# Splitting the second mixture's second-layer weights in two halves: four chunks beside the last attention batch, four in its tail

## The reference, cut to what matters

```python
x = x + L1_xattn(layernorm(x), ctx, ctx)     # 16 heads of 16: scores, softmax, values, output projection
x = x + L1_ffn(layernorm(x))                 # mixture of 8 experts, one expert per token
# inside L1_ffn, for the expert idx of each token:
h = gelu(x @ W1[idx] + b1[idx])              # W1: 8 x 256 x 512
o = (h @ W2[idx] + b2[idx]) * score          # W2: 8 x 512 x 256
```

## Time and profile before

| | |
|---|---|
| three timed runs | 1160.39, 1146.82, 1158.53 us (median 1158.53) |
| profiled execution, its own time | 1146.98 us |
| its span in the trace | 1145.2 us |
| PE, DVE, ACT, POOL busy | 85%, 65%, 42%, 25% of the span |
| chain that ended last | PE 49%, DVE 27%, DMA 10%, ACT 6% |
| mean granted TensorE clock | 0.919 of full |
| last attention batch and its tail, gate and routing | about 914 to 1040 us of the span |

### The profile page before, as it was taken

How to read it: one execution, slowest core, us unless ns; L and a number is a source line. 1 busy time by engine, 2 the same in 40 slices (tenths; PEclk the granted TensorE clock), 3 DMA queues, 4 the chain that set the end, 5 groups by cost and what they waited for, 6 DMA issues and landing times.

```text
span 1145.2 us, 20649 instructions
## 1 busy us (share of the span) xinstructions
PE 975.3 (85%) x6905; PEld 588.1 (51%) x6905; DVE 742.6 (65%) x1952; ACT 478.4 (42%) x1055; POOL 283.5 (25%) x248
## 2 busy tenths in 40 slices
PE   6878789878898799999998876888989897877993
PEld 3555455646465388878885432333333332335662
DVE  3474677684978766666663467687677856446665
ACT  3443725442343334433442310446665666532331
POOL 0334434523320233444321111100010011112551
PEclk8999989997998899999999997779998998887997
DMA  9442020003435311111114486323073014061225
GB/s 290 148 129 95 16 72 4 19 1 92 130 110 166 128 65 51 48 53 49 52 40 147 122 148 122 74 39 75 2 120 65 3 57 128 20 201 34 79 76 175
DMA packets 69506, 98.64 MB, mean 86 GB/s; under 512 B 6528, under 2 KB 56960, under 8 KB 66976
## 3 DMA queue, kind: packets, MB, share of 16 engines
q1 hardware_dynamic: 59808, 62.18, 19.0%
q0 software_dynamic: 9600, 35.14, 12.0%
HBM read 70.10 MB, written 27.13 MB: 85 GB/s over the span
## 4 chain that ended last, share of the span: by engine, by line
PE 49%; DVE 27%; DMA 10%; ACT 6%; issue 4%; POOL 2%; SPq 1%; DVEq 0%; POOLq 0%; ACTq 0%
PE pb L993 11%; PE pb L1010 7%; DVE MX L1932 5%; PE pb L1098 4%; PE pb L1011 3%; DMA QS<-qd 3%; PE pb L1122 3%; PE pb L758 2%; PE pb L1076 2%; PE pb L827 2%; PE pb L781 2%; PE pb L837 2%; DMA xr<-rows,gi 2%; DVE TQ L1541 1%; PE pb L1153 1%
## 5 line engine op out<-in xcount | busy, mean ns | idle before, releaser
L1355 ACT ACTIVATE m<-pb,b1m 128x128 f32<-128x128 f32 x404 | 115.1, 368 | 172.2 <-PE pb L993 172.1
L1932 DVE TENSOR_REDUCE MX<-pb 128x1 f32<-128x512 f32 x256 | 158.6, 684 | 43.7 <-PE pb L1076 43.3
L1412 ACT ACTIVATE EX<-pb 128x512 f32<-128x512 f32 x256 | 136.9, 598 | 115.4 <-PE pb L1122 114.5
L993 PE MATMUL pb<-xt,w1h 128*128 128x128 f16 x1616 | 157.6, 221 | 3.9 <-issue 2.7
L1010 PE MATMUL pb<-w,mh 128*128 x404 | 149.5, 380 | 5.4 <-DVE ml L1843 4.9
L752 PE MATMUL pb<-identh 128*128 128x512 f16 x558 | 136.6, 401 | 15.5 <-DVE UZ L1577 8.8
L993 PEld LDWEIGHTS pb<-xt,w1h 128*128 x1616 | 120.3, 98 | 42.5 <-issue 6.1
L993 PE MATMUL pb<-xt,w1l 128*128 128x128 f16 x808 | 112.8, 221 | 0.0
L1011 PE MATMUL pb<-w,ml 128*128 x404 | 110.2, 273 | 0.0
L2144 POOL DMA_INDIRECT outs<-ob,di x62 | 61.4, 990 | 174.3 <-DVE ob L1858 174.3
L752 PEld LDWEIGHTS pb<-identh 128*128 128x128 f16 x558 | 55.4, 102 | 87.4 <-issue 18.9
(11 more groups left out here) (319 smaller groups left out, 1598.0 us busy)
## 6 DMA issues: line engine op xcount, KB each, us to landing
SR<-in_w1m SPq DMA_DIRECT2D x20, 512.0 KB, 4.3
SR<-in_w2m SPq DMA_DIRECT2D x14, 512.0 KB, 4.8
GB<-outs SPq DMA_DIRECT2D x12, 512.0 KB, 6.9
KS<-kd SPq DMA_DIRECT2D x48, 128.0 KB, 5.6
QS<-qd POOLq DMA_DIRECT2D x24, 256.0 KB, 10.1
SRW<-in_w2m SPq DMA_DIRECT2D x10, 512.0 KB, 5.3
kd<-KHL POOLq DMA_DIRECT2D x8, 512.0 KB, 6.6
vd<-VAB POOLq DMA_DIRECT2D x4, 1024.0 KB, 4.4
```

The lines of the kernel that those rows point to most:

```text
L993: ins = pe.matmul(k.ap[:, h4 * TOK:(h4 + 1) * TOK], wt[:, bass.ds(regs[j], 128)], M.xt[j % 2][:, xc, :], start=i == 0, stop=i == 5)
L1355: ins = act.activation(M.m32[x % 2][:, h4, :], k.ap[:, h4 * TOK:(h4 + 1) * TOK], M.func, bias=M.b1[:, bass.ds(reg + 4 * g + h4, 1)], scale ...
L1412: act.activation(EX[m % len(EX)][:, i, :], k.ap, ACT.Exp, scale=0.25).then_inc(k.out, 1)
L1932: v.tensor_reduce(mx[:, t, 2 * s + j:2 * s + j + 1], k.ap, AX.X, ALU.max).then_inc(k.out, 1)
```

## The change

The chunks of `o` are taken in another order: those of w_1_2 and w_1_3 first, then those of w_1_0 and w_1_1. The first four use only the two staging buffers of the even batches, and go beside the last attention batch, behind the split `n` (nine steps: one to start and two for each chunk). SP waits for the last attention output only ahead of the fifth chunk. The other four begin after eight steps of the tail of batch 3, where the whole split began after two before.

```diff
--- before.py
+++ after.py
@@ -390,13 +390,16 @@
         def shaped(buf, like):
             return buf if len(like.shape) == 2 else buf.rearrange("p (e n) -> p e n", e=like.shape[1])
 
+        def back_first(xs):
+            return xs[len(xs) // 2:] + xs[:len(xs) // 2]
+
         def turn(n, k):
             return [i % k for i in range(n)]
 
         splits = dict(a=(cut(*W1x, a["W1T"].rearrange("p c n -> p (c n)")) + cut(*W2x, a["W2T"].rearrange("p c n -> p (c n)")), SR0, turn(4, 3)),
                       m=(blocks(E0.w1h, E0.w1l, a["w1m0"]), SR + SRS, turn(8, 3) + [3, 4, 5, 0, 1, 2, 5, 0]),
                       p=(blocks(E0.w2h, E0.w2l, a["w2m0"]), SRW + SR, [4, 5, 3, 0, 1, 2, 4, 5, 3, 0, 1, 2, 0, 1, 2, 0]),
-                      n=(blocks(E1.w1h, E1.w1l, a["w1m1"]), SR1, turn(8, 2)), o=(blocks(E1.w2h, E1.w2l, a["w2m1"]), SR2, turn(8, 4)))
+                      n=(blocks(E1.w1h, E1.w1l, a["w1m1"]), SR1, turn(8, 2)), o=(back_first(blocks(E1.w2h, E1.w2l, a["w2m1"])), SR2, [0, 1, 0, 1, 2, 3, 0, 1]))
 
         chunk_dma, chunk_at, slot_of, loaded_chunks, split_chunks = {}, {}, {}, {}, 0
         for tag in "ampno":
@@ -494,7 +497,7 @@
                 for b in bs:
                     yield from p["gate"](b)
 
-            tails = {}
+            tails, down = {}, p["split"]("o")
             for b in range(NB):
                 if 1 <= b < NB - 1:
                     p["load_half"](b + 1, 1)
@@ -504,14 +507,11 @@
                 beside(p["attend"](b, tails),
                        (chain(tails[b - 1] if b else nothing(), p["load_v"](b + 1) if 1 <= b < NB - 1 else nothing(),
                               p["qprep"](b + 2) if b + 2 < NB else nothing(),
-                              p["split"]("n") if last else nothing()), 1.0 if b else 1.3),
+                              chain(p["split"]("n"), islice(down, 9)) if last else nothing()), 1.0 if b else 1.3),
                        (gates(range(NB - 1)) if last else chain(nothing() if b else m0, p["maxima"](b + 1, b + 2 if b + 2 < NB else None)),
                         1.1 if b else 1.6))
             p["attend_done"]()
-            down = p["split"]("o")
-            for _ in range(2):
-                next(tails[NB - 1])
-            next(down)
+            weave(islice(tails[NB - 1], 8))
             beside(chain(tails[NB - 1], gates([NB - 1])), (down, 0.3), drain=False)
             p["route"](R1)
             ex = p["experts"](E1)
@@ -584,19 +584,21 @@
                         w.wait_ge(*lo_token("m", (12, 13, 15)[i]))
                     if tag == "p" and i == 3:
                         w.wait_ge(sem("x1"), NB)
+                    if tag == "o" and i == 4:
+                        w.wait_ge(bO.banks[0][2], bO.base[0] + 4 * NB)
                     if turns[i] in turns[:i]:
                         w.wait_ge(*lo_token(tag, i - 1 - turns[i - 1::-1].index(turns[i])))
                     src = chunks[i][0]
                     buf = ring[turns[i]][:, :]
                     load(slot_of[tag, i], shaped(buf, src), src)
 
-                ahead = 3 if tag in "mp" else len(ring)
+                ahead = 3 if tag in "mp" else 2 if tag == "o" else len(ring)
                 if tag == "m":
                     w.wait_ge(sem("x1"), 1)
                 if tag == "n":
                     w.wait_ge(bO.banks[0][2], bO.base[0] + 4 * (NB - 1))
                 if tag == "o":
-                    w.wait_ge(bO.banks[0][2], bO.base[0] + 4 * NB)
+                    w.wait_ge(*lo_token("n"))
                 for i in range(ahead):
                     fetch(i)
                 yield
```

## The result

| | before | after |
|---|---|---|
| median of 20 runs each, us | 1149.16 | 1151.57 |
| lowest to highest, us | 1135.84 to 1160.39 | 1143.12 to 1164.28 |
| profiled execution, us | 1146.98 | 1147.96 |
| its span, us | 1145.2 | 1146.2 |
| its mean granted clock | 0.919 | 0.922 |

The ratio after to before is 1.0055, 95% interval 1.003 to 1.008: 6.3 us slower, between 3.4 and 9.2. Measured a second time, beside later experiments, the unchanged kernel gave 1.0015 [0.9987, 1.0043]; weighted by their intervals the two give about 1.0037, or 4.3 us slower. The ratio is that of the fast runs alone, without those over 1.5% above the fastest of the same kernel; over all 20 runs of each the medians differ by 2.4 us. So the change gains nothing and most likely costs a few us, far less than 2%; the second comparison alone can't tell it from no change.

A forecast was written before the change was run, and what follows sets the result against it. PE was taken to hold 49% of the chain of waits, with no engine always busy. Waits +8.0, clock +2.5 and tail -5.6 gave +4.9 us, put on a median of 1152.8: 1157.7 us, range 1146 to 1168.

The forecast's parts named there:

- First wait: Last attention batch: the first high part waits for its load, delaying the gate's LayerNorm and XQ; cost 4.5 us.
- Second wait: Last attention batch: the fourth chunk, requested after the second low part, delays the second XT by 8.0 us; 3.5 us further cost.
- Clock: Attention: PE idles some 3 us twice and drops to a lower clock for a while; cost 2.5 us.
- Tail: From the last attention output to the routing: XTR no longer stands behind a chunk; -5.6 us, between -4 and -7.
- up to the last LayerNorm: Tail: the projection begins at the fill's end, less a low part now ahead of the LayerNorm; gain 2.5 us.
- the second XT: Tail: the high part between the two XT goes, leaving the second set by PE's transposes; gain 0.9 us.
- up to the logits: Tail: the last high part runs during L1178 and its low part ends before the logits come; gain 1.1 us.
- the low part ahead of V: Tail: this low part goes from ahead of V; gain 1.1 us.
- the projection: Tail: its 16 matmuls begin at the fill's end and take 4.5 us at the upper clock, or 5.5.
- That attention hides most of it: Rival, 15%: XQ and the second XT slip without PE, leaving the tail and some 2 us of waits; -3.6, 1149 us.
- That the lower clock stays: Rival, 25%: the two waits drop PE to 1.2 GHz until attention ends, a 9.3 us clock term; +11.7, 1164.5 us.
- That the tail does not get what it was promised: Rival, 10%: the fifth and sixth loads land late between the adds, leaving 3.1 of 5.6 us; +7.4, 1160.2 us.

The follow-up runs named there:

- e3: The changed kernel with two chunks instead of four beside the last attention batch and six from its tail on; 1.0058 of the kernel before.
- e5: The changed kernel with two pauses ahead of the first chunk, so the first load is not waited for by the gate; 0.9988 of the kernel before.
- e1_early: The changed kernel with two more staging buffers and earlier requests, so the first four chunks have their data in time; 1.0018 of the kernel before.
- e2_tail_only: The kernel before with only the tail's edit: the split begins after eight steps of the tail instead of two; 0.9966 of the kernel before.
- e9_placed: The changed kernel with each split step at a chosen place: two chunks late in attention, five in the tail, one behind the routing; 0.9941 of before.
- e10_short_fill: As e9_placed, with 4 fill matmuls on PE instead of 14 ahead of the last projection; 0.9878 of the kernel before, 0.9897 when repeated.
- e4: The changed kernel with pauses that put the same four chunks in later places, where their loads should have landed; 1.0001 of the kernel before.
- e11: As e10_short_fill, with the seventh chunk's low part moved from ahead of the copy of the logits to behind M; 0.9907 of the kernel before.

## Why the prediction was wrong, point by point

*First wait: right.* Forecast 4.5 us; XQ came 4.52 us later (11.63 against 7.11). The load landed 3.91 us after its request, the high part waited 2.84 us for it.

*Second wait: right in its place, a little smaller.* The second XT is 7.6 us late where 8.0 were forecast, and the load landed in 3.57 us after the low part that freed its buffer, where I took 3.9. I had said that the third chunk costs nothing; ACT waited 2.04 us for it, but ahead of a first XT that itself was waiting for PE another 1.54 us, so it did cost nothing. The two waits are not two terms of a sum, though: attention loses 7.8 us with the first alone (e3), 9.1 with the second nearly alone (e5) and 11.4 with both, so taking one away gives back 3.6 or 2.3 us.

*Clock: the mechanism right, the size short.* Forecast 2.5, measured 3.8 us (19.78 against 15.99 from XT to the end). The clock neither came back after one group, as my 1.5 us lower bound had it, nor stayed at the lower level as in the rival: it was low from 985 to 995 us, came back, and was low again from 998.7 to 1001.9, with one more wait of PE in between (0.80 us for an exponential); I had one spell in mind. The page of the Trainium skill that I weighed (TensorE: Matmul & The Clock Gate, Part 1), by which the clock goes back to full once PE is kept busy, would have made it the 1.5 us. The trace of after agrees with it only in that the clock returned at 995 with PE busy since 990.7; that of e5 disagrees, with PE busy for all of 999.9 to 1010.0 us and the clock at 0.50 throughout.

*Tail: right in its place, the size short.* Forecast -5.6, measured -8.1 (-6.9 in the second profile). By terms, with the chains before and after: up to the last LayerNorm 2.5 forecast and 4.0 measured (15.3 us behind the last output before, 11.3 after), the second XT 0.9 and 0.95, up to the logits 1.1 and 2.1 (0.9 in the second profile), the low part ahead of V 1.1 and 1.1. The mis-sized term is the projection: it took 3.62 us for sixteen matmuls, where I had 4.5 to 5.5 from the earlier trace rows. The 5.5 was the pace at the lower clock; before, PE waited 2.38 and 0.68 us for XTR, and the granted clock read 0.53 from 1010.74 to 1014.00 us, while after PE came in from the fill without a pause and kept the upper clock, in every profile with this order. But 4.5 was too much at the upper clock as well: it is four times a group of 1.13 us, and the sixteen in a row took 0.23 us each at the same clock, since each matmul begins before the one ahead of it has ended. At the logits the four L1180 took 1.89 us instead of 3.43, but 3.49 in the second profile, so that part is not a gain to count on. Against it the low part ahead of the logits was not hidden: it stretched to 2.31 us.

*The sum in stages: +4.9 forecast, +3.2 and +4.6 by the stages, +6.3 [3.4, 9.2] by the timed runs.* Its two misses (attention 0.9 us, tail 2.5 us) partly cancel.

*The last step failed, the one from the sum to the time.* "That execution is at the lower end: the three timed ones are 1146.82, 1158.53 and 1160.39, two levels 12 us apart", so "I put the forecast on" a median of 1152.8. With the profiled execution mixed in, the forecast of +4.9 us became 1157.7, which stands below the 1158.53 given as the time before: a slowdown written down as a number that reads as a small gain. The runs show no two levels: 20 runs of the kernel before lie between 1135.84 and 1160.39, with 1149.16 in the middle, and those of after as evenly between 1143.12 and 1164.28. The median of the three, 1158.53, is 9.4 us above that of the 20, which is more than the whole effect, and no run bears out the base of 1152.8 mixed from four; the shift should have been put on the given median (1163.4), or the text should have said that the number's place beside 1158.53 means nothing and the +4.9 is the forecast. On the median of 20, the sum gives 1154.1 against 1151.57 measured. That the measured time lies within 1146 to 1168 all the same is luck of the width, not of the base: the range was as wide as the scatter of the runs.

*The rivals.* That attention hides most of it is refuted: PE waited 2.71 us for XQ, 1.22 and 1.76 for the exponentials, and e1_early, with the data in time, got 7.9 us back. That the lower clock stays is refuted in its full size: 3.8 of 9.3 us; e5, with 5.0 us and the clock low up to 3 us ahead of the last output, comes nearest. That the tail does not get what it was promised is refuted: ACT waited 0.80 and 0.53 us for the fifth and sixth loads behind XTR, and the projection was not held up. The bias load behind two chunks on SP's queue showed no cost (gi to end 105.67 against 105.65 us, two profiles of a stage that scatters by more).

*Where the loss could have gone.* e2_tail_only keeps 6.9 us of the gain and pays nothing in attention; e9_placed shows that attention can take two chunks for nothing in its last stretch. The best version is e10_short_fill, at 0.9878 and 0.9897 in two comparisons, 12 to 14 us below before. In its traces 11.0 us of that lie between n and gi.

## What to carry to other kernels

Before work is moved beside a tight stage, look for when its data can be there and for who stands behind it in each engine's order: a buffer that is refilled only after its last use makes a load of 4 us a stall for the whole stage, and a low part of 1.2 us ahead of a small, awaited operation costs PE a wait too (e4). When a wait on the chain goes, cost the matmuls behind it at the upper clock, by their pace in a row and not by the length of a short group, and look at once at what was put there to cover the wait: here a fill of 14 had become the bound, and cutting it to 4 was worth another 2.2 us. Put a forecast shift on the same base that it will be compared with.

## What the runs showed of the hardware

- *Vector beside GpSimd.* The low part (two inputs, 128x1024) takes 1.22 us alone, 2.31 us beside GpSimd's subtraction in seven profiles of six kernels, 2.71 in three profiles of two more, and 1.22 again once moved away (e11). In all ten it begins 0.89 us behind the start of the subtraction and ends 1.08 us behind its end, though the subtraction took 2.11 us in seven and 2.52 in three: in e10 the subtraction ends at 1019.96 and the low part at 1021.04. So it looks as if the low part had waited for the subtraction to end, rather than run at a lower pace beside it; what it loses (1.09 and 1.49 us) is then about what was left of the subtraction. GpSimd's subtraction, begun first, takes the 2.11 us that it takes alone also with the low part of 2.31 us behind it (2.11 to 2.12); where it begins beside a low part it takes 2.52 (e9, e10 twice, e11). The Trainium skill (Advanced Engine Details and Errata, Miscellaneous Facts, GPSIMD Details) says that the two engines share a read and a write interface, and that instructions of Vector with two inputs conflict; the trace agrees.
- *Clock behind a wait.* After the change PE waited 1.76, 2.71 and 1.22 us within some 14 us, and the granted clock was 0.50 from 985 to 995 and again from 998.7 to 1001.9 us. A busy PE did not bring it back at once: in e5 it was 0.50 from 999.9 to 1010.0 us with PE busy all the time. In the tail, a fill of 4 matmuls directly ahead of the projection left PE at the upper clock as well as one of 14. The same tail reached the reduction of the last gate at either level, 1.89 or 3.49 us for four L1180 in two profiles of one kernel; what decides it is open.
- *The experts' part has two lengths.* From gi to the end the profiles show 105 to 107 us in six and 111 to 113 in the other six; the same changed kernel shows both (105.67 and 112.76). They sort by when they were taken: short are before, after and e1 to e4, long all of the later comparisons, on two other chips. There the kernel before, which was not profiled again, took 1154.72 and 1155.34 us (medians), against 1149.16 and 1145.72 in the first two comparisons. Much of the difference is PE waiting for gathered rows, 3.5 to 4.9 us in the short and 6.5 to 10.0 in the long; here before, then after again (waits view from gi on: us in total, times, longest):

```profile
PE pb L976 <- DMA xr<-rows,gi: 3.6, 6, 1.0
PE pb L978 <- DMA xr<-rows,gi: 6.9, 8, 1.1
```

Why the gathers took longer there is open. The difference is as large as the effect studied, and is why the stages were compared and not the spans.
